# Two layers of attention and mixture of experts in one kernel: which queue stores the result tiles

## Chip, cores and metric

One core of a Trainium2 chip runs the kernel. The metric is the device time of one execution in microseconds. The core has TensorE (PE in the profile; its weight loads PEld), VectorE (DVE), ScalarE (ACT), GpSimd (POOL) and SyncE (SP). SP issues most of the transfers here; GpSimd issues the indirect ones. In the profile "SPq" marks what a queue's own sequencer does, such as issuing a transfer.

## The reference, cut to what matters

The input x has 8 x 256 rows of 128 values, all float32. Each of two layers is half an expert block, an attention block and the other half of the same expert block (top 2 of 8 experts); every block takes a layer norm of x:

```python
for ffn, attn in ((L0_ffn, L0_attn), (L1_ffn, L1_attn)):
    x = x + 0.5 * ffn(layernorm(x))
    x = x + attn(layernorm(x))
    x = x + 0.5 * ffn(layernorm(x))

def ffn(x):                             # rows of 128 values
    xn = rms_norm(x, norm_scale)
    ids, weights = top2(xn @ w_router.T)
    u, gate = split(w_up[ids] @ xn)     # 256 columns each in layer 0, 352 in layer 1
    return sum(w_down[ids] @ (u * silu(gate)) * weights) + x
```

The attention of layer 0 is a gated one with relu squared. That of layer 1 is a causal linear attention with elu + 1; its kernel form needs an Exp on ScalarE.

## The kernel before

The 2048 rows are four groups of 512. The four expert blocks are four phases over all groups (`s` = 0 to 3; 0 and 1 belong to the first layer), and each phase of a group is 15 tiles of 128 routed rows: 240 tiles, one "slot" each. The tiles of one phase and group are cut into "rounds" of 4, 4, 4 and 3 tiles, 64 rounds in all. A router picks two experts for every row and gives each pick a place in a list sorted by expert, with each expert's part padded to whole tiles. For that, GpSimd scatters the normalised rows into `rows_dram` in that order (L422).

Per tile, SP loads that tile's expert weights four slots ahead (`load_up`, L349), after reading the expert's number into a register (L348). Per round, SP loads the routed rows (`load_rows`, L335) and TensorE transposes them (L880); ScalarE copies the transposed rows out of the bank (`rows_T`, L498). TensorE multiplies with the up weights (L865 in the first layer, L872 in the second), ScalarE does Silu (L493), VectorE multiplies (L587), and two slots later TensorE multiplies with the down weights (L826, L828) into one of two `y` banks. At the end of a round ScalarE copies the bank to one of four `y_tile` buffers (`store_y`, L486), raising `y_done`. SP waits for `y_done` and stores the tile to `y_dram` (L357, L358), raising `y_stored` of that buffer.

GpSimd's gather (L433 to L438) waits for the stores of all four rounds of a group's phase and brings two result rows per input row to `y_rows`; VectorE combines them with the residual (L619). After phases 0 and 2 the attention of that group follows (of the first or the second layer), and before each next phase its normalisation, routing and scatter, all worked in small steps between other groups' tiles (`chains`). In the last phase SP waits for the combine and stores the output (L368).

Every engine runs its own instruction list in program order, written out by a loop over slots; all ordering between engines is by semaphores. A copy into a `y_tile` buffer first waits until the store of four rounds before has landed (L485). In SP's slot the order is weight load, result store, row load, then the output store. In ScalarE's slot it is Silu, copy of results, `rows_T`, then the steps of attention and routing. An Exp in the second layer's attention (L540) makes ScalarE load another activation table, and a tiny Silu right after it (L541) loads the usual one again.

Of the kernel before, what the change touches and what calls it, by code (L numbers as in the profile page):

```python
# [22 lines left out]
P = 128  # L23
# [27 lines left out]
ROUNDS = [(s, g, a, min(4, TILES[g] - a)) for s in range(4) for g in range(NG) for a in range(0, TILES[g], 4)]  # L51
ROUND_AT = [START[s][g] + a - 2 for s, g, a, n in ROUNDS]
END_ROUND = [START[s][g] + a + n for s, g, a, n in ROUNDS]
# [2 lines left out]


DOWN = 2
STORE = 3
GATHER = 3  # L60
COMBINE = (10, 14, 9, 9)
T_AT = (10, None, 9, None)
# [18 lines left out]
def chains(t):  # L81
    return [(s, b, t - end_of(s, b)) for s in range(-1, 4) for b in range(NB) if 0 <= t - end_of(s, b) < SPAN]
# [47 lines left out]
def after(eng, sem, count):  # L130
    if count > 0:
        eng.wait_ge(sem, count)


def macaron(nc, x, up0, down0, up1, down1a, down1b, router, norm, att0_w, att0_qk, att0_out, att0_cols,
            att1_w, att1_out, bias_rows, out):
    ctx = ExitStack()
    with ctx:
        def sb(name, cols, dt=F32, rows=P):
            return ctx.enter_context(nc.sbuf_tensor(name, [rows, cols], dt))  # L140

        def sem(name):
            return ctx.enter_context(nc.semaphore(name))
# [17 lines left out]
        ysb = [sb(f"y_tile{i}", NT) for i in range(4)]  # L161
# [80 lines left out]
        y_d = [nc.dram_tensor(f"y_dram{g}", [TILES[g] * P, P], F32, kind="Internal").ap() for g in range(NG)]  # L242
# [12 lines left out]
        y_stored = [sem(f"y_stored{i}") for i in range(4)]  # L255
# [10 lines left out]
        down_done, y_done = sem("down_done"), sem("y_done")  # L266
# [17 lines left out]
        def xs(t, b, at=0, n=NT):  # L284
            return t[:, b * NT + at:b * NT + at + n]

        def tiles(ap, cols=P):
            return ap.rearrange("p (t c) -> p t c", c=cols)
# [7 lines left out]
        def gidx(s, g):  # L296

            return NG * s + g + 1
# [4 lines left out]
        @block.sync  # L303
        def _(sp):
            def load_x(b):
                sp.dma_start(tiles(xs(X, b)), x[b * NT:(b + 1) * NT, :].rearrange("(t p) d -> p t d", p=P)).then_inc(x_loaded[b], 16)

            def store_zeros(g):
                view = xg_d[g].rearrange("(p t) d -> p t d", p=P)
                for a in range(0, TILES[g], 4):  # L310
                    n = min(4, TILES[g] - a)
                    sp.dma_start(view[:, a:a + n, :], tiles(zeros[:, 0:n * P])).then_inc(zero_stored[g], 16)

            load_x(0)
            sp.dma_start(wn[:, :], norm).then_inc(norm_loaded, 16)
            sp.dma_start(wr[:, :], router).then_inc(norm_loaded, 16)
            sp.wait_ge(zeros_ready, 1)
            store_zeros(0)
            load_x(1)
            sp.dma_start(dn0[:, :], down0).then_inc(down_loaded, 16)  # L320
            load_x(2)
            load_x(3)
            sp.dma_start(stage[:, :], bias_rows).then_inc(bias_loaded, 16)
            for dst, src in ((w_hid, att0_w), (w_qk, att0_qk), (w_o0, att0_out), (cols0, att0_cols), (w_qkv, att1_w), (w_o1, att1_out)):
                sp.dma_start(dst[:, :], src).then_inc(small_loaded, 16)

            for g in range(1, NG):
                store_zeros(g)

            def load_rows(r):  # L330
                s, g, a, n = ROUNDS[r]
                sp.wait_ge(scattered[g], 16 * 2 * CH[g] * (s + 1))
                if r >= 4:
                    sp.wait_ge(s2_free, S2_TURN["rows", r - 4])
                sp.dma_start(tiles(xg[r % 4][:, 0:n * P]), xg_d[g][a * P:(a + n) * P, :].rearrange("(t p) d -> p t d", p=P)).then_inc(rows_loaded[r % 4], 16)  # L335

            def load_up(n):

                s, g = PHASE[n]
                l = LAYER[s]  # L340
                w = 2 * HIDDEN[l]
                a = n - START[s][g]
                if a == 0:
                    sp.wait_ge(eid_ready, gidx(s, g))
                if n >= RING:
                    sp.wait_ge(gate_done, n - RING + 1)
                    after(sp, up_done, n - RING + 1 - 2 * STEPS)
                v = sp.value_load(eid[g][0:1, a:a + 1], min_val=0, max_val=E - 1)  # L348
                sp.dma_start(upW[n % RING][:, 0:w], (up0, up1)[l][:, bass.ds(v * w, w)]).then_inc(up_loaded[n % RING], 16)  # L349

            def slot(t):
                if 0 <= t + AHEAD < SLOTS:
                    load_up(t + AHEAD)
                for r in range(len(ROUNDS)):
                    if END_ROUND[r] + STORE - 1 == t:
                        s, g, a, n = ROUNDS[r]
                        sp.wait_ge(y_done, r + 1)  # L357
                        sp.dma_start(y_d[g][a * P:(a + n) * P, :].rearrange("(t p) d -> p t d", p=P), tiles(ysb[r % 4][:, 0:n * P])).then_inc(y_stored[r % 4], 16)  # L358
                for r in range(len(ROUNDS)):
                    if LOAD_AT[r] == t:  # L360
                        load_rows(r)
                if t == 32:
                    sp.dma_start(dn1a[:, :], down1a).then_inc(down1_loaded, 16)
                    sp.dma_start(dn1b[:, :], down1b).then_inc(down1_loaded, 16)
                for s, b, o in chains(t):
                    if s == 3 and o == COMBINE[s]:
                        sp.wait_ge(x_done, NB * 3 + b + 1)
                        sp.dma_start(out[b * NT:(b + 1) * NT, :].rearrange("(t p) d -> p t d", p=P), tiles(xs(X, b))).then_inc(out_stored, 16)  # L368

            for t in range(FIRST_SLOT, END_SLOT):  # L370
                slot(t)
            sp.wait_ge(out_stored, 16 * NB)
# [100 lines left out]
        def _(act):  # L473
# [7 lines left out]
            def store_y(r):  # L481
                n = ROUNDS[r][3]
                act.wait_ge(down_done, r + 1)
                if r >= 4:
                    act.wait_ge(y_stored[r % 4], 16 * (r // 4))  # L485
                act.activation(ysb[r % 4][:, 0:n * P], Y[r % 2][:, 0:n * P], ACT.Copy).then_inc(y_done, 1)  # L486

            def silu(n):
                l = LAYER[PHASE[n][0]]
                w = CHUNKS[l] * P  # L490
                act.wait_ge(gate_done, n + 1)
                src = U[UP_BANK[n, "both" if l == 0 else "gate"] % 3][:, 0:w]
                act.activation(hid[n % 4][:, 0:w], src, ACT.Silu).then_inc(silu_done, 1)  # L493
# [52 lines left out]
            def slot(t):  # L546
                if 0 <= t < SLOTS:
                    silu(t)
                for r in range(len(ROUNDS)):
                    if END_ROUND[r] + DOWN - 1 == t:  # L550
                        store_y(r)
                for r in range(len(ROUNDS)):
                    if ROUND_AT[r] == t:
                        rows(r)
                for s, b, o in chains(t):
                    if s in (0, 2):
                        for j in t_stages(s, o):
                            attention(s // 2, j, b + 1)
                    if s < 3:
                        route(s + 1, b, o - route_at(s))  # L560
                if t == 1:
                    act.wait_ge(bias_loaded, 16)
                    act.activation(brows[:, :], stage[:, :], ACT.Copy).then_inc(bias_hi, 1)
# [514 lines left out]
```

## Time and profile before

| what | value |
|---|---|
| three runs, median | 757.38 us |
| three runs, lowest and highest | 756.64 and 761.06 us |
| the profiled execution, its own time | 756.74 us |
| its span, first to last instruction | 755.0 us |
| TensorE busy | 620.7 us (82%) |
| VectorE busy | 383.2 us (51%) |
| GpSimd busy | 314.8 us (42%) |
| ScalarE busy | 237.6 us (31%) |
| moved by DMA | 133.16 MB, 176 GB/s over the span |

The table is read like this. The profiled execution is one run, and its span is 1.7 us shorter than its time. Busy shares are averages over stages that have different limits, so they don't say alone what a change is worth. Issuing a transfer is not counted as busy time of an engine.

### The profile page before, as it was taken

What the parts mean: (1) busy time and instruction counts of PE and PEld (TensorE: products, weight loads), DVE (VectorE), ACT (ScalarE), POOL (GpSimd) and SP (SyncE); (2) the same over time, 40 slices, a digit from 0 to 9 for tenths busy, and PEclk for the clock granted to TensorE, in tenths of its full rate; (3) what the DMA queues carried; (4) which work ended last, traced back from release to release, by engine and by line L of the source; (5) the groups of instructions that cost most, each with busy time, mean ns of one, the idle gap of its engine ahead of it and who ended that gap; (6) DMA issues with size and microseconds to landing.
All of it is one profiled execution on the core that took longest, in us unless ns stands there. A gap on an engine that the chain in (4) does not pass through costs nothing.

```text
span 755.0 us, 15336 instructions
## 1 busy us (share of the span) xinstructions
PE 620.7 (82%) x4600; PEld 560.2 (74%) x4600; DVE 383.2 (51%) x1385; ACT 237.6 (31%) x468; POOL 314.8 (42%) x350
## 2 busy tenths in 40 slices
PE   1197869799899898858989899997997997897980
PEld 1187758678778697758989787885885785797980
DVE  4264454534646445545746636548548548452231
ACT  1043323232434333314333252341342241233330
POOL 3531724517145170675637236128128128044304
PEclk9998979889899998979999999999999999998995
DMA  9565746535546355657978766564564554676741
GB/s 312 160 210 170 223 136 207 170 95 167 166 122 199 105 173 169 204 160 232 298 213 259 199 181 170 132 177 128 145 177 142 149 160 127 188 198 203 240 135 52
DMA packets 114401, 133.16 MB, mean 176 GB/s; under 512 B 10930, under 2 KB 77490, under 8 KB 114068
## 3 DMA queue, kind: packets, MB, share of 16 engines
q1 hardware_dynamic: 106132, 115.39, 52.3%
q0 software_dynamic: 8192, 16.79, 7.6%
q8 instruction: 42, 0.69, 0.4%
q14 instruction: 35, 0.29, 0.1%
HBM read 103.04 MB, written 29.10 MB: 175 GB/s over the span
## 4 chain that ended last, share of the span: by engine, by line
PE 45%; DVE 16%; issue 15%; POOL 12%; DMA 7%; ACT 4%; POOLq 1%; SPq 0%; DVEq 0%; ACTq 0%
PE up_gate L872 14%; PE y L826 7%; PE up_gate L865 7%; POOL rows_dram L422 7%; POOL y_rows L438 4%; DMA rows<-rows_dram 3%; DVE x_res L619 2%; DVE hidden L587 2%; PE side L880 2%; PE y L828 2%; DMA rows_dram<-rms_out,rows_of 2%; DMA y_dram<-y_tile 1%; DVE attn_xT L771 1%; PE side L896 1%; PE side L964 1%
## 5 line engine op out<-in xcount | busy, mean ns | idle before, releaser
L587 DVE TENSOR_TENSOR hidden<-up_gate,hidden 128x256 f32<-128x256 f32 (+1 forms) x240 | 117.0, 489 | 258.7 <-ACT hidden L493 137.0
L438 POOL DMA_INDIRECT y_rows<-y_dram,rows_of x128 | 130.8, 1022 | 171.2 <-DMA y_dram<-y_tile 137.2
L872 PE MATMUL up_gate<-rows_T,up 128*128 128x128 f32 x1440 | 188.9, 281 | 4.7 <-ACT hidden L493 2.5
L493 ACT ACTIVATE hidden<-up_gate 128x256 f32<-128x256 f32 (+1 forms) x240 | 104.9, 437 | 276.8 <-PE up_gate L872 151.1
L872 PEld LDWEIGHTS up_gate<-rows_T,up 128*128 128x128 f32 x1440 | 174.8, 195 | 16.2 <-issue 6.6
L422 POOL DMA_INDIRECT rows_dram<-rms_out,rows_of x128 | 127.7, 998 | 92.9 <-DVE rows_of L701 56.0
L865 PE MATMUL up_gate<-rows_T,up 128*128 128x128 f32 x960 | 139.6, 292 | 2.5 <-issue 1.3
L865 PEld LDWEIGHTS up_gate<-rows_T,up 128*128 128x128 f32 x960 | 128.1, 205 | 9.3 <-issue 6.3
L826 PE MATMUL y<-down,hidden 128*128 x480 | 78.4, 289 | 8.2 <-DVE hidden L587 8.2
L880 PE MATMUL side<-ident,rows 128*128 128x128 f32 x240 | 40.5, 292 | 47.9 <-DMA rows<-rows_dram 41.7
L826 PEld LDWEIGHTS y<-down,hidden 128*128 128x128 f32 x480 | 67.9, 204 | 9.0 <-issue 9.0
L826 PE MATMUL y<-down_a,hidden 128*128 x480 | 74.1, 277 | 0.0
L498 ACT ACTIVATE rows_T<-side,norm 128x512 f32<-128x512 f32 x64 | 42.2, 660 | 89.0 <-PE side L880 89.0
L880 PEld LDWEIGHTS side<-ident,rows 128*128 128x128 f32 x240 | 29.9, 150 | 50.1 <-DMA rows<-rows_dram 43.2
L826 PEld LDWEIGHTS y<-down_a,hidden 128*128 128x128 f32 x480 | 64.2, 195 | 0.0
L486 ACT ACTIVATE y_tile<-y 128x512 f32<-128x512 f32 x64 | 36.5, 571 | 40.7 <-PE y L828 28.0
L828 PE MATMUL y<-down_b,hidden 96*128 x240 | 46.8, 276 | 0.0
L454 POOL TENSOR_TENSOR attention<-attention 128x512 f32<-128x512 f32 x16 | 17.3, 1079 | 69.7 <-DVE attention L753 69.5
L414 POOL TENSOR_TENSOR b_rstd<-b_var,minus_half 128x8 f32<-128x8 f32 x16 | 26.7, 1672 | 36.9 <-DVE b_var L603 36.5
L828 PEld LDWEIGHTS y<-down_b,hidden 96*128 96x128 f32 x240 | 36.9, 193 | 0.0
L445 POOL TENSOR_TENSOR a_rstd<-a_var,minus_half 128x4 f32<-128x4 f32 x8 | 8.2, 1026 | 62.1 <-DVE a_var L599 41.7
L619 DVE SCALAR_TENSOR_TENSOR x_res<-y_rows,w_first,x_res 128x128 f32<-128x128 f32 x64 | 18.2, 346 | 24.2 <-DMA y_rows<-y_dram,rows_of 24.2
(151 smaller groups left out, 624.5 us busy)
## 6 DMA issues: line engine op xcount, KB each, us to landing
up<-in_up SPq DMA_DIRECT2D x120, 352.0 KB, 3.8
up<-in_up SPq DMA_DIRECT2D x120, 256.0 KB, 3.3
rows<-rows_dram SPq DMA_DIRECT2D x48, 256.0 KB, 3.8
y_dram<-y_tile SPq DMA_DIRECT2D x48, 256.0 KB, 3.2
rows_dram<-zeros SPq DMA_DIRECT2D x12, 256.0 KB, 4.6
rows<-rows_dram SPq DMA_DIRECT2D x16, 192.0 KB
y_dram<-y_tile SPq DMA_DIRECT2D x16, 192.0 KB, 2.1
rows_dram<-rms_out,rows_of POOLq DMA_INDIRECT x128, 3.2
```

The costliest lines, as they stand in the source:

```text
L422: pool.indirect_dma_start(out=xg_d[g], out_offset=bass.IndirectOffsetOnAxis(ap=pos[g][:, at:at + 1], axis=0), in_=xs(Z, GROUPS[g][c // TB] ...
L438: pool.indirect_dma_start(out=gath[b % 2][:, (TB * k2 + c) * P:(TB * k2 + c + 1) * P], out_offset=None, in_=y_d[g], in_offset=bass.Indirec ...
L486: act.activation(ysb[r % 4][:, 0:n * P], Y[r % 2][:, 0:n * P], ACT.Copy).then_inc(y_done, 1)
L493: act.activation(hid[n % 4][:, 0:w], src, ACT.Silu).then_inc(silu_done, 1)
L498: act.activation(xgT[r % 3][:, 0:n * P], S[2][:, 0:n * P], ACT.Copy, scale=wn[:, LAYER[s]:LAYER[s] + 1]).then_inc(s2_free, 1)
L587: dve.tensor_tensor(h, u, h, ALU.mult).then_inc(mult_done, 1)
L619: last = dve.scalar_tensor_tensor(xs(X, b, c * P, P), gath[b % 2][:, (TB * k2 + c) * P:(TB * k2 + c + 1) * P], wk[:, c:c + 1], xs(X, b, c ...
L826: last = pe.matmul(y, hid[n % 4][:, c * P:(c + 1) * P], w, start=(c == 0), stop=(l == 0 and c == 1))
L828: last = pe.matmul(y, hid[n % 4][0:96, 2 * P:3 * P], dn1b[:, bass.ds(v * P, P)], start=False, stop=True)
L865: last = pe.matmul(U[q % 3][:, i * P:(i + 1) * P], upW[n % RING][:, at:at + P], rows_, start=True, stop=True)
L872: last = pe.matmul(U[q % 3][:, c * P:(c + 1) * P], upW[n % RING][:, at + c * P:at + (c + 1) * P], rows_, start=True, stop=True)
L880: last = pe.transpose(S[2][:, c * P:(c + 1) * P], xg[r % 4][:, c * P:(c + 1) * P], ident[:, :])
```

## The change

The store of a result tile is issued by ScalarE's queue in place of SP's. It stands right behind the copy, in ScalarE's slot `END_ROUND + 1`; SP had it in slot `END_ROUND + 2`. ScalarE waits for its own `y_done` before it issues, so that the copy's bytes are written. Nothing else moves: the buffers, the semaphores that the store raises and its shape are as before.

```diff
@@ constants
 DOWN = 2
-STORE = 3
 GATHER = 3
@@ block.sync, slot(t)
                     load_up(t + AHEAD)
                 for r in range(len(ROUNDS)):
-                    if END_ROUND[r] + STORE - 1 == t:
-                        s, g, a, n = ROUNDS[r]
-                        sp.wait_ge(y_done, r + 1)
-                        sp.dma_start(y_d[g][a * P:(a + n) * P, :].rearrange("(t p) d -> p t d", p=P), tiles(ysb[r % 4][:, 0:n * P])).then_inc(y_stored[r % 4], 16)
-                for r in range(len(ROUNDS)):
                     if LOAD_AT[r] == t:
                         load_rows(r)
@@ block.scalar, store_y(r)
                 act.activation(ysb[r % 4][:, 0:n * P], Y[r % 2][:, 0:n * P], ACT.Copy).then_inc(y_done, 1)
+                s, g, a, n = ROUNDS[r]
+                act.wait_ge(y_done, r + 1)
+                act.dma_start(y_d[g][a * P:(a + n) * P, :].rearrange("(t p) d -> p t d", p=P), tiles(ysb[r % 4][:, 0:n * P])).then_inc(y_stored[r % 4], 16)
```

## Rows read from the trace of the kernel before

**Rows 1.** The page's chain that ended last, share of the span by engine

```profile
PE 45%; DVE 16%; issue 15%; POOL 12%; DMA 7%; ACT 4%; POOLq 1%; SPq 0%; DVEq 0%; ACTq 0%
```

**Rows 2.** Waits: engine, line, waited for: total us, times, longest us

```profile
PE side L880 <- DMA rows<-rows_dram: 41.7, 8, 16.8
...
PE up_gate L872 <- ACT hidden L493: 2.5, 4, 1.3
```

**Rows 3.** Waits of SP's own queue, same columns

```profile
SPq L358 <- ACT y_tile L486: 140.3, 55, 4.9
...
SPq L335 <- DMA rows_dram<-rms_out,rows_of: 44.0, 9, 10.5
SPq L368 <- DVE spare L626: 43.8, 4, 16.7
```

**Rows 4.** The tile y_tile: duration ns min/median/max, first and last start us

```profile
L486 ACT ACTIVATE y_tile<-y x64: 491/597/599, 47.8 to 734.7; 128x512 f32<-128x512 f32 x48, 128x384 f32<-128x384 f32 x16
L358 SPq DMA_DIRECT2D y_dram<-y_tile x64: 359/382/1373, 48.5 to 735.2; - x64
...
DMA to landing us min/median/max: 2.0/2.5/5.2
```

**Rows 5.** The chain in order of time: start us, us, what

```profile
73.12 2.06 DMA y_dram<-y_tile
...
650.24 5.76 DMA rows<-rows_dram
...
705.10 3.01 DMA y_dram<-y_tile
```

**Rows 6.** Timeline, 324 to 334 us: start us, us, engine line op [idle before]

```profile
324.38 0.60 ACT L486 ACTIVATE y_tile<-y 128x512 f32<-128x512 f32 x1
...
333.66 0.47 SPq L358 DMA_DIRECT2D y_dram<-y_tile  x1
```

**Rows 7.** Timeline, 446 to 452 us

```profile
446.79 0.49 ACT L486 ACTIVATE y_tile<-y 128x384 f32<-128x384 f32 x1 [0.85 <-PE y L828]
447.30 1.28 ACT L540 ACT_TABLE_LOAD   x1
...
451.17 0.94 PE L872 MATMUL up_gate<-rows_T,up 128*128 128x128 f32 x6 [1.30 <-ACT hidden L493]
```

**Rows 8.** Line 540: duration ns min/median/max, first and last start

```profile
L540 ACT ACT_TABLE_LOAD  x4: 1283/1283/1283, 447.3 to 610.6; - x4
```

**Rows 9.** Timeline, 151 to 153 us

```profile
151.57 0.38 SPq L358 DMA_DIRECT2D y_dram<-y_tile  x1
...
151.81 0.69 ACT L498 ACTIVATE rows_T<-side,norm 128x512 f32<-128x512 f32 x1 [0.26 <-PE side L880]
152.55 1.88 PE L896 MATMUL side<-router,z_T 128*128 128x8 f32 x8 [0.78 <-ACT rows_T L498]
```

**Rows 10.** Timeline, 243 to 247 us

```profile
243.46 0.60 ACT L486 ACTIVATE y_tile<-y 128x512 f32<-128x512 f32 x1 [1.07 <-PE y L826]
...
243.96 0.68 ACT L498 ACTIVATE rows_T<-side,norm 128x512 f32<-128x512 f32 x1
...
244.69 1.06 PE L896 MATMUL side<-router,z_T 128*128 128x8 f32 x8 [0.83 <-ACT rows_T L498]
...
246.85 1.11 PE L915 MATMUL side<-ident,attention 128*128 128x128 f32 x4 [1.10 <-DVE attention L608]
```

**Rows 11.** Timeline, 399 to 402 us

```profile
399.14 0.49 ACT L493 ACTIVATE hidden<-up_gate 128x384 f32<-128x384 f32 x1
...
400.28 1.50 PE L872 MATMUL up_gate<-rows_T,up 128*128 128x128 f32 x12
```

**Rows 12.** Timeline, 648 to 650 us

```profile
648.53 0.43 SPq L358 DMA_DIRECT2D y_dram<-y_tile  x1
...
649.79 0.34 SPq L349 DMA_DIRECT2D up<-in_up  x1
```

**Rows 13.** Windows: us, busy us (count) PE, PEld, DVE, ACT, POOL, PEclk, DMA share, GB/s

```profile
736.00:737.00 1.00, 0.00 (x0) 0.00 (x0) 0.00 (x0) 0.00 (x0) 0.00 (x0) 1.00 0.70 197
```

## Prediction

> **What bounds the kernel now.** I read the page's chain of work first: 45% of it is TensorE, 16% VectorE, 12% GpSimd, 7% DMA and 4% ScalarE [rows 1]. So TensorE sets the time where it has tiles. Elsewhere the loop over a group does: result tiles stored, rows gathered, combined, routed, scattered, loaded again. Next I read who makes TensorE wait. The largest entry is the load of routed rows, 41.7 us in 8 waits. TensorE waits for a Silu of ScalarE only 4 times in the second layer, 2.5 us in all [rows 2]. Hence ScalarE has slack behind most of its copies and none at four places.
>
> Then I read the waits of SP's own queue: 55 of the 64 times SP reaches a result store it stands waiting for the copy, 140.3 us in all [rows 3]. That looks like much to win. But SP's waiting costs only if something queued behind it comes late at TensorE. SP also waits 9 times for a scatter (44.0 us) and 4 times for the final combine (43.8 us) [rows 3]; a store queued behind these leaves late.
>
> **What the store is worth.** A copy takes 597 ns and an issue on SP 382 ns (359 to 1373); it lands 2.0 to 5.2 us after, median 2.5 [rows 4]. Where SP is waiting, the issue starts 0.02 us after the copy ends: at the table-load place the copy ends at 447.28 and ScalarE's next work starts at 447.30 [rows 7]; SP's issue at the copy's end at 151.55 begins at 151.57 [rows 9]. Those 55 stores cannot leave earlier from ScalarE. Nine others come late: one copy ends at 324.98, its store goes at 333.66, 8.7 us later [rows 6]. I laid all 64 copies beside their stores: the late ones are the second or third round of a group or, once, a fraction; the last round of each of the 16 phases always leaves 0.02 to 0.03 us after its copy. GpSimd's gather waits for all four rounds, so the last one sets it. So no gather starts earlier by an earlier issue. Five stores lie on the chain of waits, three of them with 2.06 us and one with 3.01 us to landing [rows 5]; the last lands at about the minimum too. Against the minimum of 2.0 us [rows 4] only the 3.01 us has anything to give.
>
> **What leaves SP.** 64 waits and 64 issues. Behind them stand the loads of expert weights and of routed rows. Weight loads never make TensorE wait in the view of waits. Row loads mostly follow a scatter, and SP stands ready for those. One place is different: at 648.53 SP, just freed from the final combine, issues an overdue store (0.43 us), then a weight load at 649.79, and only then the row load that lands 5.76 us later, on the chain [rows 12, 5]. With the store gone the row load goes 0.43 us sooner, and I count -0.45 with the gap. The bytes of that store also leave this stretch. Alone, a store filled 0.70 of one microsecond of all DMA engines [rows 13], so the relief is between 0 and -0.7. A later overdue store (copy ends at 653.03) moves to an earlier moment of the same row load and can cost the same 0 to +0.7. I cancel the two. Two more overdue stores move next to a row load that TensorE awaits (at 98 and at 692 us, 0 to +0.7 each), and one moves out of the way of a scatter (688 us, 0 to -0.7); these I take at zero together, bounds -1.4 to +2.1 for all five. For the 3.01 us landing a queue of its own may give 0 to -1.0; I take -0.5.
>
> The Trainium skill (DMA: Bandwidth & Descriptors, section Issuing engines are not separate DMA queues) says that DMAs from all issuing engines run on the same 16 DMA engines and that spreading them saves only the sequencer's issue time. By it the -0.5 would be 0 and the sum half a microsecond higher. No row of the kernel before has ScalarE issuing, so nothing here shows it.
>
> **What arrives on ScalarE.** After each copy it now waits for that copy's end, issues (median 0.38 us by SP's row, the nearest), and only then goes on. The wait also ends the overlap of two activations: a copy of rows_T starts at 243.96 although the result copy runs until 244.06 [rows 10]. I take 0.40 us where ScalarE went on at once and 0.55 us where it overlapped. Queued behind are Silu, rows_T, Tanh and the Exp of attention. Place by place:
> - Second layer, Silu right behind. In the dense stretch a Silu runs 399.14 to 399.63. The bank that it frees is wanted in the second half of the up matmuls that start at 400.28, about 400.95 [rows 11]. That is 1.3 us of slack against 0.4 to 0.55 us: nothing. If the slack were gone, each of some dozen places would cost up to 0.4 us.
> - First layer: the Silu starts about 0.3 us behind the copy anyway, so the delay is 0.1 to 0.2 us. Nothing.
> - rows_T right behind, with TensorE's scores waiting for it: scores start at 244.69 and take 1.06 us, then TensorE idles until 246.85 for a VectorE result that doesn't need them [rows 10]. A delay of 0.55 us goes into that idle 1.10 us. A second place (198 us) is alike. At 151.81 rows_T starts only 0.24 us behind SP's issue and TensorE's scores follow at 152.55 [rows 9]; ScalarE would be free at 151.57 + 0.38 + 0.05 = 152.00, so +0.2 us, on the chain.
> - The Exp of attention. The table load starts at 447.30, 0.02 us behind the copy. Exp, a second table load and Silu follow, and TensorE idles 1.30 us for that Silu at 451.17 [rows 7]. There are four such places [rows 8] and they are all four of TensorE's waits for Silu [rows 2]. Nothing covers them: 4 x 0.40 = +1.6 us.
> - The copy itself still waits for the store four rounds earlier to land; stores never leave later than before, so this gains or loses nothing.
>
> **Sum.** +1.6 + 0.2 - 0.45 - 0.5 = +0.85 us. The profiled execution took 756.74 us (span 755.0 and 1.7 us around it), so 757.6 us. The median of the runs shown is 0.64 above that execution, so 758.2; I put 758.0. It is a change that cannot be told from none: this kernel's measurement tells about 1%, or 7.6 us.
>
> **The rivals.**
> - *Dear issue on ScalarE* (the slower side, chance 0.10). The unknown is what an issue costs there. The nearest rows reach to 1373 ns on SP [rows 4]. At 1.4 us the four attention places cost 5.6 us, the place at 152 us 1.2 us, and the two covered ones show 0.4 us each: +7.6 us and none of the gains, 764 to 765 us. From about 1.3 us each issue exceeds also the slack behind the second layer's copies [rows 11], and from 1.4 us the result is slower by 1%. For it: the long issues came while GpSimd also issued. Against: the median of 64 is 0.38. The Trainium skill (Perfetto Trace Analysis, section DMA Instruction, HWDGE) says that an issuing sequencer first waits for a lock on a shared descriptor generator; a store on ScalarE could then wait for a load of SP that used to stand in the same queue. No row here shows two such sequencers.
> - *SP set free pays* (chance 0.13). The row load at 650 us gains 0.45 + 0.7, the scatter at 688 us 0.7, the landing at 705 us 1.0, and the delays on ScalarE go into idle time: about -2.9 us, 753.8 to 754.5 us. For it: 140.3 us of waiting on SP [rows 3]. Against: TensorE's waits hang on scatters, and the attention places have no cover.
> - *Overdue stores collide with row loads* (chance 0.07): all bounds on the dear side, 0.85 + 2.1, and the landing gain gone: +3.5 us, 760 to 761 us.
>
> **Chances and range.** The forecast (755.5 to 759.8) gets 0.70. 80% of the cases lie between 754.5 and 763.0 us, which takes in the gains' bound nearly and the cheaper part of the dear issue. The three runs of before alone span 756.6 to 761.1, so I go no narrower. Faster by over 1% needs twice and more of what all the gains give, 0.02. Slower by over 1% takes the dear issue at its worst row, 0.05. Within 1%: 0.93.
>
> **What the profile after would show.** Issues of y_dram on ScalarE's queue, 64 of them, each 0.02 to 0.1 us behind its copy with 0.36 to 0.5 us duration; if they last over 1 us, the dear rival holds. SP's wait for the copy gone, and its waits for TensorE longer by about as much: SP is paced by TensorE either way. TensorE's waits for Silu still 4, but 4.1 us rather than 2.5. The row load near 650 us issued 0.45 us closer to the out store. GpSimd's waits for y_dram unchanged within a few us. The forecast is wrong if TensorE's waits for ScalarE appear at more than these places, or if its waits for row loads shrink by several microseconds.

## The result and the profile after

The change makes the kernel slower by 1.4%, about 11 us.

| | before | after |
|---|---|---|
| median of four runs each | 757.56 us | 768.53 us |
| lowest and highest | 756.64, 761.06 | 767.15, 771.36 |
| ratio, 95% interval | | 1.0141 [1.0098, 1.0184] |
| profiled execution, its span | 756.74, 755.0 us | 768.52, 766.7 us |

A later set with the same kernel gave 1.0141 again. The forecast was 758.0 us, "within 1%", with 754.5 to 763.0 as its range. Its sum of +0.85 us was on the slow side, as the result is, but it is a thirteenth of the size, and one of its terms, the landing, had the wrong sign.

The page of the kernel after, its span and the chain by engine. DMA has 9% of the chain where it had 7% [rows 1], ScalarE 5% where it had 4%.

```profile
span 766.7 us, 15336 instructions
...
PE 43%; DVE 17%; issue 13%; POOL 12%; DMA 9%; ACT 5%; POOLq 1%; ACTq 0%; SPq 0%; DVEq 0%
```

The tile y_tile after (duration ns min/median/max, first and last start). An issue on ScalarE costs 366 ns and never more than 422, less than on SP. But the landing has gone from a median of 2.5 us to 3.8 [rows 4]. The trace has the landing of 32 of the 64 stores before and of 48 after. Of the same 16 stores, the third of each phase goes from 3.24 to 3.74 us and the last of each phase from 2.06 to 3.63.

```profile
L483 ACTq DMA_DIRECT2D y_dram<-y_tile x64: 366/366/422, 50.2 to 746.8; - x64
...
DMA to landing us min/median/max: 2.0/3.8/5.7
```

Two places of the timeline show what has changed (start us, us, engine line op, idle before). The first is the last store of a group's phase, the one on which GpSimd's gather hangs. Before:

```profile
211.89 0.49 ACT L486 ACTIVATE y_tile<-y 128x384 f32<-128x384 f32 x1
212.40 0.38 SPq L358 DMA_DIRECT2D y_dram<-y_tile  x1
213.54 0.34 SPq L349 DMA_DIRECT2D up<-in_up  x1
215.44 1.09 POOL L438 DMA_INDIRECT y_rows<-y_dram,rows_of  x1 [16.60 <-DMA y_dram<-y_tile]
```

and after:

```profile
217.27 0.49 ACT L480 ACTIVATE y_tile<-y 128x384 f32<-128x384 f32 x1
217.53 4.64 SPq L348 DMA_DIRECT2D up<-in_up  x2
217.79 0.37 ACTq L483 DMA_DIRECT2D y_dram<-y_tile  x1
...
222.10 1.09 POOL L432 DMA_INDIRECT y_rows<-y_dram,rows_of  x1 [17.43 <-DMA y_dram<-y_tile]
```

In both the store follows its copy's end by 0.02 to 0.03 us. Before, SP stood waiting for that copy, so the next weight load could start only 1.14 us behind the store, and the gather began 3.04 us behind it. After, SP is not held: its weight load (256 KB) goes out at 217.53, before the copy is even finished, and the store's 192 KB (three tiles of 128 x 128 in float32) run beside it on the same DMA engines. The gather begins 4.31 us behind the store. Over the 16 phases of the groups the last store lands in 2.06 us (median) before and in 3.63 after, in all but one with a weight load issued 0.12 to 0.43 us ahead of it. One store checks this: the very last, at 746.84, has no load beside it and lands in 2.04 us from ScalarE's queue (2.03 before, from SP's). On the chain of work (start us, us, what) the five stores of before take 2.06, 2.06, 2.06, 3.01 and 2.03 us, 11.2 us in all; the first and the fourth are in [rows 5], the second is the store above. After, six are on it, with 20.3 us; three of them:

```profile
217.79 3.35 DMA y_dram<-y_tile
...
717.05 4.40 DMA y_dram<-y_tile
...
746.84 2.04 DMA y_dram<-y_tile
```

The second place is ScalarE itself, at a slot of the second layer in which rows_T, Silu, the multiply and TensorE's next up matmuls all stand behind the copy:

```profile
407.76 0.60 ACT L480 ACTIVATE y_tile<-y 128x512 f32<-128x512 f32 x1 [0.85 <-PE y L825]
408.39 0.41 ACTq L483 DMA_DIRECT2D y_dram<-y_tile  x1
408.85 0.69 ACT L495 ACTIVATE rows_T<-side,norm 128x512 f32<-128x512 f32 x1 [0.49 <-ACT y_tile L480]
409.44 0.48 ACT L490 ACTIVATE hidden<-up_gate 128x384 f32<-128x384 f32 x1
...
409.95 0.56 DVE L584 TENSOR_TENSOR hidden<-up_gate,hidden 128x384 f32<-128x384 f32 x1 [1.28 <-ACT hidden L490]
...
410.78 1.49 PE L869 MATMUL up_gate<-rows_T,up 128*128 128x128 f32 x11 [0.60 <-DVE hidden L584]
```

rows_T starts 0.49 us behind the copy's end. The delay passes through Silu and through VectorE's multiply, and TensorE stands 0.60 us for that multiply, in whose bank its next results go.

The waits after (total us, times, longest). TensorE's wait for VectorE's multiply ahead of the down matmuls was 8.2 us with a longest of 5.8 before; GpSimd's wait for stores was 137.2 us in 8 waits. At the other eight gathers of before, GpSimd comes to the gather when the store has landed already. After, only five are left of these.

```profile
POOL y_rows L432 <- DMA y_dram<-y_tile: 148.4, 11, 20.5
...
PE side L877 <- DMA rows<-rows_dram: 41.0, 7, 17.0
...
PE y L823 <- DVE hidden L584: 12.1, 4, 7.2
```

With the 4600 matmuls of the two profiled executions laid beside each other, the kernel after is 11.6 us behind at the last one: 7.3 us of idle time and 4.3 us of busy time. By what TensorE waited for, after minus before:

| TensorE's waits | us |
|---|---|
| VectorE's multiply (at 97 us +1.39, 196 +1.15, 243 +1.12, 364 +1.03, 400 +0.60, 687 +0.37) | +5.6 |
| Silu, the four places behind an Exp, 0.41 each | +1.65 |
| rows_T (198 us +0.55, 245 us +0.88) | +1.6 |
| attention steps of VectorE, shorter because TensorE comes to them later | -2.2 |
| routed rows (656 us -1.58, 289 us +0.49, 695 us +0.49) | -0.7 |
| issue | +1.7 |
| no wait: TensorE's busy time, 625.0 against 620.7 | +4.3 |
| other entries | -0.4 |

The row on busy time is not safely of the change; the repeats below return to it.

### The profile page after: what moved, and what is told of

Read it like the earlier page. It is cut to its first block, busy times and chain, and to the rows that moved or that the text cites. A ratio compares the mean times of both kernels' runs of the same rounds, so it can differ in the third digit from the quotient of the medians.

```text
span 766.7 us, 15336 instructions
## 1 busy us (share of the span) xinstructions
PE 625.0 (82%) x4600; PEld 562.5 (73%) x4600; DVE 383.6 (50%) x1385; ACT 238.8 (31%) x468; POOL 315.8 (41%) x350
## 4 chain that ended last, share of the span: by engine, by line
PE 43%; DVE 17%; issue 13%; POOL 12%; DMA 9%; ACT 5%; POOLq 1%; ACTq 0%; SPq 0%; DVEq 0%
PE up_gate L869 13%; PE up_gate L862 7%; POOL rows_dram L416 7%; PE y L823 7%; POOL y_rows L432 4%; DVE x_res L616 3%; DMA rows<-rows_dram 3%; DMA y_dram<-y_tile 3%; DVE hidden L584 3%; DMA rows_dram<-rms_out,rows_of 2%; PE side L893 2%; PE side L877 2%; PE y L825 2%; ACT rows_T L495 1%; PE side L961 1%
## 5 line engine op out<-in xcount | busy, mean ns | idle before, releaser
L439 POOL TENSOR_TENSOR a_rstd<-a_var,minus_half 128x4 f32<-128x4 f32 x8 | 8.2, 1028 | 61.2 <-DVE a_var L596 40.8
```

## The experiments

Two theories, A and B in the expectations. *Late landing*: SP's wait for the copy was a brake on its weight loads; without it a load goes ahead of the store on which the gather hangs, and each group's loop is longer by the later landing. *Busy ScalarE*: wait and issue on ScalarE delay what stands behind the copy, at more places than the four that I had counted. A third thing to exclude, C, is that ScalarE's queue itself is slow.

Four sets of four kernels ran, each beside the kernel before on the same chip. Sets 1 and 3 fell on two chips on which every execution, of the kernel before too, takes 16 to 18% longer (881 and 894 us), so only their landings, not their per cents, are read against the result. That choice was made after set 1, where ratios of 0.992 and 0.994 agreed with no theory; the kernel after itself did not run on either chip, so what it would have cost there is not known. TensorE's mean granted clock is 0.89 and 0.87 in the profiles of before there, against 0.94 here. The line below is of the kernel before in set 1: ScalarE stands 120 us until a release that the trace gives to no instruction of this core. The kernel before on the usual chip has no such entry.

```profile
ACT hidden L493 <- remote: 120.4, 21, 10.8
```

### Holding SP back as before, store still on ScalarE

```diff
  (the kernel after, in SP's slot between weight load and row load)
+                for r in range(len(ROUNDS)):
+                    if END_ROUND[r] + 2 == t:
+                        sp.wait_ge(y_done, r + 1)
```

> The changed kernel (store on ScalarE), and SP again waits for the copy at the place where it used to store, but issues nothing there. Theory A (the transfers that SP held back behind its wait now run ahead of the store): the store of a phase's last round lands in a median of about 2.1 us again (2.06 before, 3.63 in the changed kernel), and the time falls to the kernel before's plus the four table-load places of 0.41 us and some rows_T delays: 1.5 to 4 us above before. Theory B (what ScalarE does for wait and issue costs the time): nothing changes, about 11 us above before. Theory C (ScalarE's queue lands slower as such): landing stays at 3.6 us and the time stays about 11 us above before.

Set 1: 0.9992 [0.9943, 1.0041] of before; the last store of a phase lands in 2.07 us again.

> The changed kernel with SP waiting for the copy at its old place, once more, because on the chip of the first set ScalarE stood still for long stretches that belong to no kernel and hid a per cent. Theory A (transfers no longer held back by SP run ahead of the store): a phase's last store lands in 2.1 us, the time is 1.5 to 4 us above before. Theory B (ScalarE's wait and issue): about 11 us above. Theory C (ScalarE's queue as such): landing 3.6 us, about 11 us above.

Set 2: 763.12 us (761.15 to 765.92) against 757.64, ratio 1.0069 [1.0041, 1.0096], +5.2 us. Theory A had given 1.5 to 4 us, B and C about 11: the wait alone, with nothing issued, gives back half of the loss. Its timeline at the same place:

```profile
215.92 0.49 ACT L483 ACTIVATE y_tile<-y 128x384 f32<-128x384 f32 x1
216.44 0.37 ACTq L486 DMA_DIRECT2D y_dram<-y_tile  x1
...
217.15 3.67 SPq L348 DMA_DIRECT2D up<-in_up  x2
...
219.47 1.08 POOL L435 DMA_INDIRECT y_rows<-y_dram,rows_of  x1 [16.66 <-DMA y_dram<-y_tile]
```

The store is 0.71 us ahead of the load, and the gather starts 3.03 us behind it, as before, though ScalarE's queue carries it. So that queue is not slow. At one place holding back does not restore what was. In the second of the 16 phases SP has two loads of down weights behind its wait. They went out 0.42 us and more behind the store before; here the first goes out at the same instant as the store:

```profile
116.05 0.34 SPq L360 DMA_DIRECT2D down_a<-in_down1a  x1
116.05 0.42 ACTq L486 DMA_DIRECT2D y_dram<-y_tile  x1
...
124.06 1.08 POOL L435 DMA_INDIRECT y_rows<-y_dram,rows_of  x1 [23.70 <-DMA y_dram<-y_tile]
```

The gather starts 8.01 us behind this store, against 3.10 before and 4.56 after. TensorE's next wait for normalised rows is 5.23 us, against 4.09 before and 3.66 after. So some 1.1 us of the 5.2 that stay is a landing as well. The rest goes with ScalarE: TensorE's waits for Silu (2.5 us before [rows 2]) and for the multiply (8.2 us) are still up.

```profile
PE up_gate L872 <- ACT hidden L493: 4.1, 4, 1.7
...
PE y L826 <- DVE hidden L587: 9.1, 4, 6.0
```

### The same store on SP, but behind the next weight load

```diff
-STORE = 3
+STORE = 4
```

This is the kernel before with one number changed: SP stores in slot `END_ROUND + 3`, so one more weight load stands ahead of the store in its queue; ScalarE issues nothing.

> The kernel before with SP's store one slot later, so that the weight load of the next slot is issued ahead of it; ScalarE does nothing more than before. Theory A: the store of a phase's last round lands in 3.3 us or more, TensorE waits as in the changed kernel except at the table loads, and the time is 5 to 10 us above before. Theories B and C: the store is only issued up to 0.5 us later, the time is within 3 us of before.

Set 1: 0.9924 [0.986, 0.9988], though the medians of all runs are 882.82 us against 881.28; the last store of a phase lands in 3.52 us. By its ratio this pointed the other way.

> The kernel before with SP's store one slot later, behind the next weight load, once more on another chip. Theory A: last stores land in about 3.5 us, time 5 to 10 us above before. Theories B and C: within 3 us of before.

Set 2: 762.70 us (757.38 to 768.08), 1.0057 [1.0028, 1.0087], +4.3 us (2.1 to 6.6 by the interval; theory A had given 5 to 10, the others under 3). Landing of the 48 stores that have one in the trace, and the place that answers to the ones above:

```profile
DMA to landing us min/median/max: 2.0/3.9/6.0
```
```profile
213.17 4.41 SPq L349 DMA_DIRECT2D up<-in_up  x2
...
216.99 0.49 ACT L486 ACTIVATE y_tile<-y 128x384 f32<-128x384 f32 x1
...
217.63 0.43 SPq L358 DMA_DIRECT2D y_dram<-y_tile  x1
...
221.71 1.08 POOL L438 DMA_INDIRECT y_rows<-y_dram,rows_of  x1 [18.56 <-DMA y_dram<-y_tile]
```

The two load issues grouped in the first row end at 217.58, just ahead of the store: the gather lags 4.08 us. The last stores land in 3.61 us (median), the figure of the kernel after (3.63), on SP's own queue. Its waits for Silu stay where they were:

```profile
PE up_gate L872 <- ACT hidden L493: 2.5, 4, 1.3
```

So late landing costs 4.3 us by itself, with no part of ScalarE in it. Its way to TensorE can be read here too. At 200 us TensorE stands for VectorE's multiply; VectorE works without a break up to it from `rms_out`, which waited for GpSimd. That GpSimd was late because its gathers start later is read from the order of its work and was not measured apart:

```profile
195.36 1.12 DVE L608 TENSOR_SCALAR rms_out<-x_res,b_meanvar,b_rstd 128x128 f32<-128x128 f32 x4 [2.24 <-POOL b_rstd L414]
...
200.21 0.84 PE L826 MATMUL y<-down,hidden 128*128 x4 [1.88 <-DVE hidden L587]
```

The kernel after has the same pair at 196.90 us (2.12 us for GpSimd) and 201.75 us (1.88 us for the multiply). In the kernel before VectorE comes to `rms_out` without a wait, and TensorE stands 0.73 us.

### A wait and an issue on ScalarE, stores left on SP

```diff
  (the kernel before, in store_y behind the copy)
+                act.wait_ge(y_done, r + 1)
+                act.dma_start(probe_d[r * 16:(r + 1) * 16, :], zeros[0:16, 0:P]).then_inc(probe_stored, 16)
```

The small transfer (16 pieces of 512 bytes here, 128 of 16 bytes in set 1) goes to a scratch area that nothing reads; ScalarE waits for its end after the last slot.

> The kernel before, with its store on SP, and in addition ScalarE waits for its copy and issues a small transfer (128 x 4 values of zeros to a scratch tensor of its own) where the changed kernel issues the store. Theory A: only ScalarE's own delays are paid, 1.6 us at the table loads and up to 2 us at rows_T: 1.5 to 4 us above before. Theory B: about 11 us above before. Theory C: as A.

Set 1: 0.9935 [0.99, 0.997]. SP's stores landed in 3.9 us (median of the 32 that have a landing in the trace; 2.3 of the same 32 in the kernel before there), though the load order was that of before: the small transfer beside them has its own price. I take it as a flaw of the probe.

> The kernel before, and ScalarE in addition waits for its copy and issues a transfer of 16 rows of 512 bytes (zeros, to a scratch tensor) where the changed kernel issues the store. The first form of this, 128 pieces of 16 bytes, made SP's store itself land in 3.7 us, so this one is smaller in pieces. If the store's landing stays near 2.1 us, theory A: 1.5 to 4 us above before. Theory B: about 11 us above. If a small transfer beside the store also raises its landing to 3 us or more, theory A expects the time to follow: 6 to 11 us above.

Set 2: 765.21 us (762.75 to 766.58), 1.0101 [1.0079, 1.0122], +7.6 us, between what A (1.5 to 4 us) and B (about 11) had given. The trace has the landing of the third store of each phase only: 3.10 us (median) against 3.24 for the same 16 stores before. The gather waits for its last store at eight places. It lags by 3.11 to 3.20 us at seven of them, against 2.96 to 3.10 before, and at the eighth by 3.69 against 3.97. So the flaw is small here. The second layer at 402 us:

```profile
402.27 0.38 SPq L360 DMA_DIRECT2D y_dram<-y_tile  x1
402.27 0.39 ACTq L490 DMA_DIRECT2D probe_dram<-zeros  x1
402.71 0.69 ACT L502 ACTIVATE rows_T<-side,norm 128x512 f32<-128x512 f32 x1 [0.47 <-ACT y_tile L488]
...
404.46 1.26 PE L877 MATMUL up_gate<-rows_T,up 128*128 128x128 f32 x9 [0.41 <-DVE hidden L592]
```

TensorE again waits 0.41 us for the multiply behind a copy with rows_T, with the stores where they were. TensorE's waits for Silu are 4.2 us in 4. The two queues issue in the same 0.4 us and neither is longer for it.

### The wait on ScalarE without an issue

```diff
  (the kernel before, in store_y behind the copy)
+                act.wait_ge(y_done, r + 1)
```

> The kernel before with one addition: ScalarE waits for the end of each result copy, and issues nothing. The second set says that wait and issue on ScalarE together cost 5 to 7.6 us. The wait alone ends the overlap of two activations (about 0.1 us) in front of rows_T and Tanh. If it is the issue's 0.37 to 0.39 us that costs, this kernel is within 2 us of before; if the drained pipeline costs most, it is 3 us or more above.

Set 3: 1.0023 [0.9989, 1.0056].

> The kernel before, and ScalarE waits for the end of each result copy and issues nothing. If the issue's 0.37 to 0.39 us costs, this kernel is within 2 us of before, and TensorE's four waits for Silu stay 2.5 us in all. If the wait and the drained pipeline cost most, it is 3 us or more above before.

Set 4: 759.25 us (756.08 to 761.52), 1.0007 [0.9984, 1.0029]; waits for Silu 2.5 us in 4, unchanged.

```profile
PE up_gate L873 <- ACT hidden L494: 2.5, 4, 1.3
```

The wait costs nothing that can be told from zero, 2.2 us at most by the interval. So ScalarE's part is in the main the issue's 0.37 to 0.39 us.

### Holding SP back only for the last store of a phase

```diff
  (the kernel after, in SP's slot)
+                    if END_ROUND[r] + 2 == t and r % 4 == 3:
+                        sp.wait_ge(y_done, r + 1)
```

> The changed kernel, and SP waits for the copy only at the 16 last rounds of a phase (of 64), where GpSimd's gather waits for the store. If it is the landing of these stores that costs, the gather starts 3.0 us behind the store again and the time is that of the kernel with all waits back, 4 to 7 us above before. If the other 48 count too, it stays near 10 us above.

Set 3: 0.9979 [0.9938, 1.002].

> The changed kernel, and SP waits for the copy at the 16 last rounds of a phase only. If the landing of these stores costs: GpSimd's gather starts 3.0 us behind the store and the time is 4 to 7 us above before. If the other 48 count too: near 10 us above.

Set 4: 762.96 us (760.21 to 766.42), 1.0063 [1.0036, 1.009]. It gives back as much as the wait at all 64 rounds (1.0069), as far as intervals of 2 us on either side can tell, with SP standing only 14.6 us for copies:

```profile
SPq L347 <- ACT y_tile L483: 14.6, 14, 1.1
```

The last stores land in 2.10 us (median) from ScalarE's queue, while those of the second and third rounds, not held, take 4.28 and 4.50. So the 16 stores that complete what a gather waits for are the ones that count; no price of the other 48 shows. The second phase is the exception again: its last store takes 8.56 us, and TensorE's wait for normalised rows is 6.33 us.

### Repeats of the two kernels

> The kernel before once more, unchanged, for a second profile of it: how much of the span comes from stretches in which TensorE runs at half pace. In the changed kernel's profile a stretch from 38 to 43 us, ahead of the first store, gave 2.2 us. If such stretches lie elsewhere in this second profile, they are no part of the change; spans of 754 to 759 us are expected.

> The changed kernel itself beside the others on the same chip: 1.0 to 1.8% above before by all theories, last stores landing in about 3.6 us.

> The kernel before unchanged, for a second profile of it on a chip of the usual kind: where TensorE runs at half pace. Three profiles of changed kernels have such a stretch from 38 to 43 us, ahead of the first store, of 1.9 to 2.9 us, and the first profile of before has not. If this one has it, the stretch is no part of the change.

> The kernel before unchanged, for a second profile on a chip of the usual kind. If it has the half-pace stretch of TensorE at 38 to 43 us, that stretch is no part of the change; span 754 to 759 us.

The repeat of the kernel before in set 1 took 878.22 us, the kernel after in set 2 took 769.38 us (765.01 to 772.89), 1.0141 [1.0109, 1.0173], with the last stores landing in 3.64 us; before took 894.44 us in set 3 and 757.88 us in set 4. The last one bears on a reading of mine. In the profile after, 16 up matmuls that took 2.03 us before take 3.63 us (227 against 127 ns each), though the granted clock of that stretch reads full:

```profile
39.81 3.63 PE L862 MATMUL up_gate<-rows_T,up 128*128 128x128 f32 x16
```

The kernel before of set 4 has such a stretch as well (3.76 us for the same 16, at 39.63), and it took 757.88 us all the same. So that stretch is no part of the change. Compared with the first profile's 620.7 us, TensorE is busy 1.5 us longer in that one, 1.4 with the issue alone, 2.8 with the wait only, 3.5 with the store late on SP, 2.6 and 4.0 in the two held-back kernels, and 4.3 and 4.7 in the two profiles of the kernel after. This differs between executions of one kernel. But both profiles of after stand above both of before, and two of each are too few to say that none of it is of the change.

### A version that beats both

The row load at 650 us stood behind SP's wait for the final combine [rows 12, 5]. Taking the store off SP relieved it only in part. So the kernel before, with its stores on SP, and the output store two steps later instead:

```diff
-                    if s == 3 and o == COMBINE[s]:
+                    if s == 3 and o == COMBINE[s] + 2:
```

> The kernel before, with the four output stores (line 368) two slots later in SP's list, so that SP doesn't stand waiting for the last combine with weight and row loads queued behind. TensorE waited 3.65 us at 656 us for a row load that left late for this reason. Expected 1 to 4 us faster than before; if the DMA engines and not SP's wait held that load, no difference.

Set 3: 0.9916 [0.988, 0.9953], without two single executions of 1085 and 1551 us for which nothing in the record gives a cause.

> The kernel before, with the four output stores (line 368) two slots later in SP's list. On the chip of the third set it was 0.8% faster (0.5 to 1.2%). Expected here 1 to 6 us faster than before: the row load that TensorE waits for at 656 us leaves sooner. If the DMA engines and not SP's wait held that load, no difference.

Set 4: 748.58 us (746.63 to 750.13) against 757.73, ratio 0.9862 [0.9835, 0.9889]: 10.5 us faster, where I had expected 1 to 6. At the place where the row load was overdue, weight load and row load are now ahead of the output store:

```profile
644.34 0.34 SPq L349 DMA_DIRECT2D up<-in_up  x1
...
644.78 0.38 SPq L335 DMA_DIRECT2D rows<-rows_dram  x1
...
648.06 0.40 SPq L368 DMA_DIRECT2D out<-x_res  x1
```
```profile
PE side L880 <- DMA rows<-rows_dram: 35.7, 8, 16.9
```

TensorE's waits for row loads fall from 41.7 us [rows 2] to 35.7: 3.65 us less at 656 us and 2.41 at 695 us. The span is 746.9 us, against 755.0 of the first profile of before and 756.2 of the one in this set. SP's wait for the combine was 43.8 us [rows 3], and relieving it paid; taking away its 140.3 us for copies did not.

## Why the prediction was wrong, step by step

**The landing: the step that failed.** I argued that the last store of each phase leaves 0.02 to 0.03 us behind its copy in either kernel, "so no gather starts earlier by an earlier issue". That was right, and I stopped there. I kept the landing at about the minimum of 2.0 us, and for the 3.01 us landing I even took -0.5. But the minimum was a product of the wait that the change removes: SP stood at the copy with nothing in flight behind it. When I listed what leaves SP, I asked only whether loads would come *late* at TensorE, never what they would collide with if they came *early*. The same store behind a load costs 3.6 us to land, on either queue. Priced alone it is +4.3 us (store behind the load on SP), where I had taken -0.5; as what holding SP back at 16 stores gives back, against the repeat of the kernel after, it is 1.0141 - 1.0063 of 757.7, 5.9 us. My bounds for bytes colliding, -1.4 to +2.1, were for overdue stores beside row loads, and none was for a load beside a store. The row that could have shown it was there: landings of 2.0 to 5.2 us with a median of 2.5 [rows 4]. In the kernel before, the last store at 212.40 us took 2.06 us while 98 GB/s moved in its first 2 us; the one at 368.70, of the same size, took 4.70 us at 357 GB/s.

The Trainium skill (DMA: Bandwidth & Descriptors, section Issuing engines are not separate DMA queues) says that all issuing engines' DMAs run on the same 16 DMA engines and that another issuer saves only issue time. The trace agrees with the first half: the very last store, alone, took 2.04 us on ScalarE's queue and 2.03 on SP's, and last stores beside a load 3.63 and 3.61. The second half is true of the issue, but it speaks of a saving alone, and this kernel lost 11 us. I weighed this rule and drew from it only that the -0.5 might be 0. The step that I missed is mine to add: transfers that one queue's wait had kept apart now share those engines, and that makes the landing term positive.

**Silu behind second-layer copies: 0 taken.** My 1.3 us of slack was that of the bank which Silu frees [rows 11]. The same up matmuls also need the bank which VectorE's multiply reads, after Silu. At places where rows_T runs between copy and Silu, that multiply is late for TensorE: 0.60 us at 410 us after (and 0.41 with the issue alone), and at the layer change at 364 us 0.55 to 0.63 in the kernels with an issue on ScalarE and the last stores as before, and 1.03 after. With the store late on SP neither place has it. I followed one reader of the bank and not the last one.

**rows_T beside TensorE's idle, places at 198 and 244 us: 0 taken.** Right as far as it went. In the kernel after TensorE waits 0.55 and 0.88 us more for rows_T and 2.2 us less for the VectorE results behind them. But VectorE's multiply at 196 and 243 us is not covered: +1.15 and +1.12 after, +0.94 and +0.66 with the issue alone, and +1.15 and +0.80 with the store late on SP and nothing issued on ScalarE. So these waits belong to both causes: in the kernel after VectorE runs without a break up to the multiply, and its wait ahead of that is for GpSimd (2.12 and 1.18 us). The small place at 152 us came as forecast: TensorE's wait for rows_T is 0.96 us where it was 0.78. Here is the rows_T place at 250 us after. I had taken a delay of 0.55 us. It is 0.87: rows_T starts 0.77 us behind the copy's end, where before it started 0.10 us ahead of it [rows 10].

```profile
250.13 0.60 ACT L480 ACTIVATE y_tile<-y 128x512 f32<-128x512 f32 x1 [2.20 <-PE y L823]
...
251.50 0.69 ACT L495 ACTIVATE rows_T<-side,norm 128x512 f32<-128x512 f32 x1 [0.77 <-ACT y_tile L480]
```

**The four Exp places: +1.6.** Right in place, count and size: 4.1 us of waits for Silu in the held-back kernels where 2.5 stood, four waits still. One of them after; the table load starts 0.44 us behind the copy and TensorE's idle is 1.72 us instead of 1.30 [rows 7]:

```profile
457.36 0.49 ACT L480 ACTIVATE y_tile<-y 128x384 f32<-128x384 f32 x1 [0.85 <-PE y L825]
...
458.29 1.28 ACT L537 ACT_TABLE_LOAD   x1 [0.44 <-ACT y_tile L480]
...
462.16 0.60 PE L869 MATMUL up_gate<-rows_T,up 128*128 128x128 f32 x3 [1.72 <-ACT hidden L490]
```

With the two terms above, ScalarE's part measures at most 4.8 to 5.2 us (SP held back, some 1 us of it a landing) or 7.6 us (issue alone), where I had 1.6 + 0.2.

**The row load near 650 us: -0.45.** Right in sign: TensorE's wait there is 1.58 us shorter, partly offset by +0.49 at each of two others. That the loads of routed rows would not shrink by several microseconds held (41.0 against 41.7).

**SP and GpSimd.** SP's wait for the copy is gone and its waits for TensorE grew from 89.0 and 77.3 us to 175.2 and 132.5, as predicted: SP is paced by TensorE. GpSimd's wait for y_dram I had called unchanged; it grew by 11.2 us and was the sign of the late landings.

**The rivals.** *Dear issue* had the right side and a false premise: the issue is 366 ns, cheaper than on SP, and the result is dearer than that rival. *SP set free pays* was the opposite of what happened: SP set free was a good part of what cost. *Overdue stores collide with row loads* had bytes in each other's way, but at row loads, and those waits did not grow. No rival held the mechanism, and so the range could not hold the time.

**What adds up and what is open.** Each cause alone gives +4.3 us (late landing) and +7.6 us (issue on ScalarE), 11.9 us together against 10.7 to 11.0 measured. The intervals of the two are about 2 us wide on either side, so the sum fits but does not pin the shares. Holding SP back splits the loss into 5.5 to 5.9 us given back and 4.8 to 5.2 left, and these two add up by construction. With SP held back at all rounds, TensorE's waits are longer by 1.64 us for Silu, 2.0 for the multiply, 1.6 for rows_T and 1.1 for normalised rows (the odd landing), of which 1.9 go into idle time: 4.5 us against 5.2. In the one profiled execution all idle time together is 2.9 us longer and the busy time 4.0, so this agreement is loose. Open: how much of TensorE's longer busy time belongs to the change; and why the issue alone costs 7.6 us and the held-back kernel 5.2. TensorE's waits marked "issue" ahead of the up matmuls are also open. They are 3.6 and 5.1 us in the two profiles of after, 4.9 with the store late on SP and 4.2 with 48 stores not held back, against 2.1 to 2.7 us in the profiles of all others on that kind of chip: they go with weight loads that run ahead, but what ends them is not in the trace. Of the 10.5 us of the faster version, 9.3 show between the two profiles of its set, 5.1 of them in waits for row loads (40.8 against 35.7 us).

## What to carry to other kernels

A queue that stands waiting is also a brake on whatever is queued behind it. Before taking the wait away, find the transfer that ends last before the next stage, note how it lands with nothing beside it, and ask which transfer will now be issued ahead of it. And when an engine that holds several banks in turn is delayed, look for the last reader of each bank that the bottleneck wants back, not for the first.

## What the runs showed of the hardware that I had not expected

- A store of 192 KB lands in 2.06 us (median) with no load issued within 1.1 us behind it, and in 3.6 us with a weight load issued 0.3 to 0.4 us before it, alike on SP's and on ScalarE's queue.
- An issue on ScalarE takes 366 ns (366 to 422), against 382 on SP (359 to 1373). At 402.27 us both queues issue at the same instant, 0.38 and 0.39 us: no wait for one another shows.
- 64 waits on ScalarE for its own copy cost nothing that can be told from zero (1.0007 [0.9984, 1.0029]), though they end the overlap of two activations.
- Sixteen up matmuls took 3.63 us in place of 2.03 at a granted clock that reads full; such stretches came in executions of the kernel before as well.
